# A graph and expert kernel: the first graph's order and magnitudes rebuilt, the last graph's sums shared out

## The reference

```
xn = layernorm(x);  H = (adj != 0);  w = adj[0, :]
D = 1/(H w);  B = 1/(column counts of H)
conv(h, W, b) = D * (H (B * (H^T (h W^T)))) + b
h  = relu(conv(xn, W1, b1))                 # 256 -> 512
h  = layernorm(h) * gamma + beta
x1 = x + conv(h, W2, b2) + xn               # 512 -> 256
x2 = layernorm(x1)
logits = x2 rw + rb;  mask = softmax over the two largest of 4
comb = sum_e mask_e * silu(x2 ew_e + eb_e)
y  = x2 + comb ow + ob
out = x1 + nw * y / sqrt(mean(y*y) + eps)
```

## Time and profile before

| what | value |
|---|---|
| median of 3 runs | 729.49 us (727.12 to 731.59) |
| the profiled execution | 727.4 us, its span 725.9 us |
| TensorE busy | 685.4 us (94% of the span) |
| VectorE busy | 622.8 us (86%) |
| ScalarE busy | 528.7 us (73%) |
| GpSimd busy | 342.7 us (47%) |
| share of the chain that ended last | PE 87%, DVE 5%, ACT 3%, DMA 1% |

### The profile page before, as it was taken

The page is one execution under the profiler, slowest core; times in us unless marked ns, Lnnn a source line. Parts: engine busy times, 40 slices in busy tenths (PEclk is TensorE's granted clock), DMA queues, the critical chain, the costliest instruction groups (busy, mean ns, idle before and its releaser), DMA issues.

```text
span 725.9 us, 15857 instructions
## 1 busy us (share of the span) xinstructions
PE 685.4 (94%) x5197; PEld 475.7 (66%) x5197; DVE 622.8 (86%) x1544; ACT 528.7 (73%) x1091; POOL 342.7 (47%) x731
## 2 busy tenths in 40 slices
PE   3777999999999999999999999999999999999982
PEld 2464485866758586775858577685857668585672
DVE  3987799898989989898989989898998989898676
ACT  4567868688696868778686877869686786967563
POOL 4142625456373545646354554635355563634433
PEclk9999999999999999999999999999999999999997
DMA  8547449575665938566583947657394756537312
GB/s 284 190 77 242 92 106 235 93 236 117 210 141 136 230 63 256 112 212 134 153 203 61 274 99 227 120 173 173 83 260 90 236 111 197 121 77 184 59 30 59
DMA packets 42591, 111.72 MB, mean 154 GB/s; under 512 B 4161, under 2 KB 5313, under 8 KB 42561
## 3 DMA queue, kind: packets, MB, share of 16 engines
q0 software_dynamic: 13536, 41.42, 32.8%
q1 hardware_dynamic: 29024, 69.92, 27.4%
HBM read 69.91 MB, written 16.25 MB: 119 GB/s over the span
## 4 chain that ended last, share of the span: by engine, by line
PE 87%; DVE 5%; ACT 3%; DMA 1%; issue 1%; POOL 1%; SPq 0%; POOLq 0%; DVEq 0%; ACTq 0%
PE bank L1310 16%; PE bank L1312 16%; PE bank L1311 16%; PE bank L1395 7%; PE bank L1396 7%; PE bank L1421 7%; PE bank L1453 4%; PE bank L1454 4%; PE bank L1364 4%; PE bank L1357 2%; PE bank L1412 2%; DMA b1b<-b 1%; PE bank L1466 1%; PE bank L1345 0%; ACT x L591 0%
## 5 line engine op out<-in xcount | busy, mean ns | idle before, releaser
L1310 PE MATMUL bank<-xth,ewh 128*128 128x512 f16 (+1 forms) x272 | 100.4, 369 | 2.6 <-DVE ewl L827 2.6
L1311 PE MATMUL bank<-xtl,ewh 128*128 128x512 f16 (+1 forms) x272 | 100.3, 369 | 0.0
L1312 PE MATMUL bank<-xth,ewl 128*128 128x512 f16 (+1 forms) x272 | 100.3, 369 | 0.0
L536 ACT ACTIVATE silu<-bank,ebcol,ksc 128x512 f32<-128x512 f32 x120 | 89.7, 769 | 7.7 <-PE bank L1312 4.0
L399 POOL TENSOR_TENSOR comb<-comb,silu 128x1024 f32<-128x1024 f32 x30 | 74.3, 2478 | 0.6 <-DVE silu L904 0.6
L1310 PE MATMUL bank<-w2h,hnth 128*128 128x256 f16 x256 | 70.3, 275 | 0.1
L1311 PE MATMUL bank<-w2l,hnth 128*128 128x256 f16 x256 | 70.2, 274 | 0.0
L1312 PE MATMUL bank<-w2h,hntl 128*128 128x256 f16 x256 | 70.2, 274 | 0.0
L926 DVE SCALAR_TENSOR_TENSOR hntl<-bank,hnth 128x512 f16<-128x512 f32 x64 | 42.7, 687 | 26.8 <-ACT hnth L554 25.6
L1453 PE MATMUL bank<-xsh,h 128*128 128x256 f16 x256 | 59.0, 279 | 3.1 <-DVE xsl L809 2.4
L904 DVE TENSOR_TENSOR silu<-silu,bank 128x1024 f32<-128x1024 f32 x45 | 54.7, 1216 | 7.9 <-ACT silu L536 7.8
(11 more groups left out here) (273 smaller groups left out, 2072.7 us busy)
## 6 DMA issues: line engine op xcount, KB each, us to landing
adjin<-adj SPq DMA_DIRECT2D x16, 1024.0 KB, 5.4
adjtin<-adjt SPq DMA_DIRECT2D x16, 1024.0 KB, 7.9
xin<-x SPq DMA_DIRECT2D x16, 512.0 KB, 7.1
xb<-xn SPq DMA_DIRECT2D x16, 512.0 KB, 4.1
xb<-x POOLq DMA_DIRECT2D x16, 512.0 KB, 8.9
xb<-b POOLq DMA_DIRECT2D x16, 512.0 KB, 5.4
xb<-vadd POOLq DMA_DIRECT2D x16, 512.0 KB, 4.5
out<-x SPq DMA_DIRECT2D x15, 512.0 KB, 4.9
```

Source lines behind the costliest of these rows:

```text
L536: af(silu[:, i % 4, :], bank[E_BANK[i]][:, :], ACT.Silu, bias=ebcol[:, i:i + 1], scale=ksc[:, 2:3]).then_inc(silu_dn, 1)
L1310: mm(outp, lh, rh, start=first, stop=False)
L1311: mm(outp, lh, rl, start=False, stop=False)
L1312: return mm(outp, ll, rh, start=False, stop=last)
```

## The change

In the opening of graph 0, SP loads adj, W1 and adjt right behind x, and gamma, W2, beta and b1 after them. TensorE starts with 18 products that nothing reads (`keep_busy`), and has two groups of 5 of them later. x is normalized and split by halves (`first_x`, `first_lo`), the aggregation takes the halves as they come (`first_aggregation`), and the column counts of H are made by TensorE as products with a column of ones (`count_products`, for graphs 0 and 1). `w2g` is made by GpSimd. The magnitudes of W1, `w2g` and the expert weights are no longer maxima: ScalarE sums absolute values in one instruction (`sum_abs`, with an accumulator); for the output and router weights VectorE takes the largest absolute value directly. The W2 scale, the fourth `z_part`, `bias_rows`, `v_part`, x of graph 1 and the expert weights' split stand elsewhere in the order; `ewh` is made in graph 0 and `ewl` ahead of `xtl` in graph 1. The steady passes keep their instructions.

In the tail, GpSimd makes y * nw for graph 14 (`yw_dn`) and ScalarE multiplies by the root (`finish`), where VectorE did both; the first half's sum over experts is one step on GpSimd and two on VectorE; the second half has two steps on GpSimd and the last one on VectorE by tiles of 128 nodes; the split, the output products and y follow by tiles. The first expert's high products stand ahead of the router.

```diff
-            for dst, src in ((bet[:, :], beta), (gam[:, :], gamma),
-                             (w2f[:, :, :], w2t.rearrange("(k p) f -> p k f", p=P))):
+            sp.dma_start(adjin[:, :, :], adj[0].rearrange("(t p) e -> p t e", p=P)).then_inc(adj_in, 16)
+            sp.dma_start(w1f[:, :, :], w1t.rearrange("(k p) h -> p k h", p=P)).then_inc(a_in, 16)
+            sp.dma_start(adjtin[:, :, :], adjt[0].rearrange("(t p) c -> p t c", p=P)).then_inc(adjt_in, 16)
+            for dst, src in ((gam[:, :], gamma), (w2f[:, :, :], w2t.rearrange("(k p) f -> p k f", p=P)),
+                             (bet[:, :], beta), (b1b[:, :], b1.to_broadcast([P, DH]))):
                 sp.dma_start(dst, src).then_inc(b_in, 16)
-            sp.dma_start(adjin[:, :, :], adj[0].rearrange("(t p) e -> p t e", p=P)).then_inc(adj_in, 16)
-            for dst, src in ((w1f[:, :, :], w1t.rearrange("(k p) h -> p k h", p=P)),
-                             (b1b[:, :], b1.to_broadcast([P, DH]))):
-                sp.dma_start(dst, src).then_inc(a_in, 16)
-            sp.dma_start(adjtin[:, :, :], adjt[0].rearrange("(t p) c -> p t c", p=P)).then_inc(adjt_in, 16)
...
             prep_x(0, again=False)
+            gp.wait_ge(b_in, 64)
+            tt(w2g[:, :, :], w2f[:, :, :], gam[:, :].unsqueeze(2).to_broadcast([P, KH, D]), ALU.mult).then_inc(w2g_dn, 1)
...
-                        gp.wait_ge(b_scale, 1)
-                    scale_dn(g)
+                        gp.wait_ge(a_scale, 1)
+                    scale_dna(g)
+                    if ffn:
+                        scale_dnb(g)
                 if prep and ffn:
...
                     if not ffn:
+                        gp.wait_ge(b_scale, 1)
+                        scale_dnb(g)
                         add_x(g)
+                        prep_x(g + 1)
                     add_b2(g)
                 if ffn:
                     add_up(f, 2)
                 if conv:
...
                 roots_y(LAST - 1, ALL, 0)
 
-                s = slice(0, T_ROW)
-                for e in range(1, NE):
-                    gp.wait_ge(comb_st, 7 * LAST + e + 1)
-                    if e > 1:
-                        gp.wait_ge(last_sum, e - 1)
-                    tt(comb[:, :, s], comb[:, :, s], last_silu(e)[:, :, s], ALU.add).then_inc(last_sum, 1)
+                gp.wait_ge(y_dn, 2 * LAST)
+                gp.wait_ge(out_st, 32 * (LAST - 1))
+                tt(yf[:, :, :], y[:, :, :], nwb[:, :].unsqueeze(1).to_broadcast([P, CT, D]), ALU.mult).then_inc(yw_dn, 1)
+
+                s0, s1 = slice(0, T_ROW), slice(T_ROW, 2 * T_ROW)
+                gp.wait_ge(comb_st, 7 * LAST + 2)
+                tt(comb[:, :, s0], comb[:, :, s0], last_silu(1)[:, :, s0], ALU.add).then_inc(last_sum, 1)
+                gp.wait_ge(comb_st, 7 * LAST + 6)
+                tt(comb[:, :, s1], comb[:, :, s1], last_silu(1)[:, :, s1], ALU.add).then_inc(last_sum, 1)
+                gp.wait_ge(comb_st, 7 * LAST + 7)
+                gp.wait_ge(last_sum, 2)
+                tt(comb[:, :, s1], comb[:, :, s1], last_silu(2)[:, :, s1], ALU.add).then_inc(last_sum, 1)
...
+            def sum_abs(col, src):
+                n = src.shape[1] * src.shape[2]
+                return af(silu[:, :, :].rearrange("p k n -> p (k n)")[:, 0:n], src[:, :, :].rearrange("p k n -> p (k n)"),
+                          ACT.Abs, accum_out=mags[:, col:col + 1])
...
+            def first_x():
+                act.wait_ge(xrs_st, 4)
+                for j in range(2):
+                    s = slice(CG * j, CG * j + CG)
+                    for t in range(CG * j, CG * j + CG):
+                        af(xn[:, t, :], xin[:, t, :], ACT.Identity, bias=xnb[:, t:t + 1],
+                           scale=xrs[:, t:t + 1]).then_inc(xn_dn, 1)
+                    act.wait_ge(xn_dn, CG * j + CG)
+                    af(xsh[:, s, :], xn[:, s, :], ACT.Copy, scale=XS).then_inc(xs_hi if j else x0_hi, 1)
...
+            first_x()
+            act.wait_ge(tables, 16)
+            act.wait_ge(a_in, 16)
+            sum_abs(W1, w1f).then_inc(a_mag, 1)
...
+                        act.wait_ge(a_mag, 1)
+                        act.wait_ge(w2g_dn, 1)
+                        sum_abs(W2, w2g).then_inc(b_mag, 1)
...
+                if conv and not ffn:
+                    hnt_part(act, g, 0)
+                    setup_hi(b_scale, ((w2g, w2h, W2),), b_hi)
+                    relu(act, g, 3)
+                    hnt_part(act, g, 1)
...
+                        act.wait_ge(b_mag, 1)
+                        act.wait_ge(c_in, 16 * 6)
+                        sum_abs(EX, ewf).then_inc(ew_sum, 1)
...
+                    else:
+                        bias_rows(act, g)
...
+                            if not ffn:
+                                prep_x(g + 1, range(e, e + CG))
...
-                    setup_hi(c_scale, ((rwf, rwh, RW), (owf, owh, OW)), c_hi)
+                    setup_hi(c_scale, ((rwf, rwh, RW), (ewf, ewh, EX), (owf, owh, OW)), c_hi)
...
-                if prep:
-                    count_edges(act, g, 1 - odd)
+                if prep and ffn:
+                    count_edges(act, g, 1 - odd, late)
...
+            def last_ct(act, h, t):
+                c = slice(T_ROW * h, T_ROW * h + T_ROW) if h == 0 else slice(P * t, P * t + P)
+                act.wait_ge(half_dn, 1 if h == 0 else t)
                 af(cth[:, :, c], comb[:, :, c], ACT.Copy, scale=ksc[:, 5:6]).then_inc(ct_hi, 1)
+
+            def finish(act, t):
+                act.wait_ge(yw_dn, 1)
+                act.wait_ge(rr_st, 2 * LAST)
+                af(yf[:, t, :], yf[:, t, :], ACT.Copy, scale=yrr[:, t:t + 1]).then_inc(yf_dn, 1)
...
+                for t in range(1, CT):
+                    finish(act, t)
+                for t in range(CG, CT):
+                    last_ct(act, 1, t)
...
+            def first_lo(j):
+                s = slice(CG * j, CG * j + CG)
+                dve.wait_ge(xs_hi if j else x0_hi, 1)
+                STT(xsl[:, s, :], xn[:, s, :], XS, xsh[:, s, :], ALU.mult, ALU.subtract).then_inc(xs_lo if j else x0_lo, 1)
...
+            def degrees(g, odd, counted_by_pe):
+
+                if counted_by_pe:
+                    dve.wait_ge(deg_rdy, g + 1)
+                else:
+                    dve.wait_ge(deg_dn, 4 * g - 4)
+                TS(dmax[:, :], bank[DEG_BANK][:, DEG] if counted_by_pe else deg[:, :], 1.0, None, ALU.max).then_inc(be_max, 1)
...
+            prep_h(0, again=False)
+            first_lo(0)
+            degrees(0, 0, True)
+            first_lo(1)
...
-                    setup_lo(c_hi, 2, ((rwf, rwh, rwl, RW), (owf, owh, owl, OW)), c_lo)
+                    setup_lo(c_hi, 1, ((rwf, rwh, rwl, RW),), c_lo)
...
+                    if not ffn:
+                        d_vector(g)
...
+                if conv and ffn and not late:
+                    setup_lo(c_hi, 2, ((ewf, ewh, ewl, EX),), c_lo)
...
-                        setup_scale_b()
-                        d_vector(g)
-                    dve.wait_ge(dn_scaled, 2 * g + 1)
+                        dve.wait_ge(b_in, 64)
+                    dve.wait_ge(dn_scaled, (2 * g if ffn else g) + 1)
...
+                    if not ffn:
+                        v.memset(spare[:, :], 0.0)
+                        h_aggr(g, 1)
+                        h_stats(g, 2)
+                        dve.wait_ge(hbn_dn, 4 * g + 3)
+                        v.memset(spare[:, :], 0.0)
+                        h_aggr(g, 2)
+                        setup_scale_b()
                     z_part(g, 3)
-                    h_aggr(g, 1)
-                    if not ffn:
...
+                    else:
+                        hnt_part(g, 0)
...
+                if conv:
+                    hnt_part(g, 3)
+                if ffn:
+                    combine_sum(f)
+                if ffn:
+                    ct_part(f, 0)
+                if conv:
+                    v_part(g, 0)
+                    if not ffn:
+                        largest(c_turn, slice(EX, RW + 1), 2, c_top)
...
+            def last_pair_up():
+                c = slice(0, T_ROW)
+                dve.wait_ge(comb_st, 7 * LAST + 4)
+                TT(last_silu(2)[:, :, c], last_silu(2)[:, :, c], last_silu(3)[:, :, c], ALU.add).then_inc(last_pair, 1)
...
+            def first_half_sum():
+                c = slice(0, T_ROW)
+                dve.wait_ge(last_pair, 1)
+                dve.wait_ge(last_sum, 1)
+                TT(comb[:, :, c], comb[:, :, c], last_silu(2)[:, :, c], ALU.add).then_inc(half_dn, 1)
...
+            def last_add(t):
+                c = slice(P * t, P * t + P)
+                dve.wait_ge(comb_st, 7 * LAST + 8)
+                dve.wait_ge(last_sum, 3)
+                TT(comb[:, :, c], comb[:, :, c], last_silu(3)[:, :, c], ALU.add).then_inc(half_dn, 1)
...
+                last_pair_up()
                 last_weigh(1, 0)
-                finish(LAST - 1, (2, 3), False, False)
+                first_half_sum()
```

(132 more changed lines are left out.)

199 lines of the change are left out of this document (70 added, 129 removed).

## The result

759.6 us (median of 4 runs, 758.4 to 760.3) against 728.8 (727.1 to 731.6): ratio 1.042, 95% interval 1.039 to 1.044. The change makes the kernel 31 us slower. The profiled execution has a span of 758.8 us, 32.9 more than before, and takes 760.3 in all.

The account below looks back on a forecast made before the run. TensorE, busy almost throughout the steady passes, was taken as the bound, so only the ends could gain: start 6.3 plus tail 0 from 727.4 gives 721.1, 723.2 on the median's scale, stated as 723.0; range 718.5 to 727.

Parts of the forecast that it names:

- nothing of the diff touches those passes: Steady passes, 75.2 to 691 us, TensorE busy 614.4 of 615.8: all new branches lie outside them, so no change there.
- The rival on the other side: Steady passes: VectorE starts them 2.6 late and never recovers, TensorE waiting in each; 737 at 1 us a pass, chance 0.05.
- the rival without locks: Opening and tail: VectorE and GpSimd don't hold each other up, 0.5 and 2.1 more gained; 720.0, chance 0.27.
- the lock of the tail: Tail: GpSimd's product `yw` holds VectorE's `mask` 2.2 us, cancelling a gain of 2.1; taken as 0, bounds -2.1 and +0.6.
- the last step of the sum: Conversion of 721.1, the profiled execution's scale, to the runs' median, 2.1 higher: 723.2, stated as 723.0.
- Opening of graph 0: Start of graph 0: shorter path to the first W1 products, at 21.7 instead of 27.02, gain 5.3.
- Lock of the opening: Opening of graph 0: GpSimd's `prep_h` may hold up VectorE's `xnb` if adj lands before 8.6; 0 to 1.0, taken 0.5.
- Loads: Opening rival: adj and adjt land at 11.5 and 17 as before, counts wait, gain only 3; 726.5, chance 0.11.
- the rival of a falling clock: Opening: TensorE's clock falls between warm-up and aggregation, which again runs slower, gain 4.3; 725, chance 0.12.
- Rest of graph 0: From W1 products to `x1_half(0)`: GpSimd's queue of additions to xb holds it; 57.27 becomes 53.5, gain 3.8.
- Graph 1: From `x1_half(0)` to graph 1's W1 products: 13.9 instead of 17.9, W1 products at 67.4, 7.8 ahead of 75.16.
- The 1.0 for VectorE's lateness: Graph 1: route and mask come 2.6 later relative to TensorE, missing transpositions; cost 1.0, bounds 0 and 2.

Follow-up runs that it names:

- e1: Changed kernel with ten instructions of waits on a reached semaphore ahead of VectorE's first instruction, its loop at 329 instead of 319: 719.3 us, ratio 0.987.
- e15: Changed kernel with VectorE's loop moved by waits to 329 and all 28 `keep_busy` products left out: 720.8 us.
- e12: Changed kernel with five wait instructions (loop at 324), GpSimd's tail product y*nwb ahead of the x2 addition, and graph 0's additions to xb issued earlier: 713.9 us.
- e8: Changed kernel with VectorE's loop moved by waits to 329 and GpSimd's tail product y*nwb put ahead of the x2 addition: 717.2 us, ratio 0.984.
- e14: Changed kernel with a single wait instruction ahead, VectorE's loop of 261 at 320: 747.4 us, with shorter pauses.
- e3: Changed kernel with 128 wait instructions ahead of VectorE's first instruction, its loop at 447: 769.7 us, with pauses.
- e11: Changed kernel with no waits ahead, VectorE's loop one instruction shorter (260) at 319: 760.9 us, with all five pauses.
- e13: Kernel before the change with 114 wait instructions ahead, VectorE's loop at 443 in the list and 447 on the engine: 774.7 us, with pauses.
- e7: Changed kernel with 261 wait instructions ahead of VectorE's first instruction, its loop at 580: 743.9 us, no pauses.

## Why the prediction was wrong

**The step that failed** is in its first paragraph: "nothing of the diff touches those passes". That holds for the operations, but for one instruction more in VectorE's loop, and between the marks e1 takes 630.8 us where the kernel before takes 634.8. But a loop has a place in the instruction stream too, and fourteen instructions less ahead of it, as the engine counts (ten in the list), moved it from a good one to a bad one. The prediction had this at nothing without a reason; it costs 41.5 us between the marks, more than everything that the forecast weighed. The rival on the other side had TensorE waiting in each pass of the loop because VectorE began late. It waited at five jumps back because VectorE's code was not there; the sign was right by accident, and the mechanism fell in e1, where VectorE begins as late and loses nothing by it. Nothing in the trace of before shows a cost of the place; what it had was the queue of instructions with only 2 of its 15 packets between 200 and 640 us (the changed kernel has 26 there), and the program's list would have given the shift.

**The rest is best read in e1**, which is the change without that accident: 719.3, at the lower end of the range and 3.7 below the forecast. It is near the rival without locks (720.0), but not by its mechanism, since the lock of the tail did bite. Some 1.6 of the 3.7 are the change: 1.8 more at the start, 0.2 less in the tail. The other 2 are in the last step of the sum, which put some 2 on top of 721.1 because the profiled execution of before lay that far under its median; in e1 the profiled execution (719.5) lies 0.2 over it.

- *Opening of graph 0*: W1 products at 21.14 in the changed kernel and 21.29 in e1 (forecast 21.7). Counts, aggregation at 11.18 and at 0.11 spacing were right. Of the half microsecond, 0.4 is an error of addition: the prediction's own steps behind 15.6 add up to 21.3.
- *Lock of the opening*: 0.5 was taken off for it and should not have been. `prep_h` did hold a GpSimd instruction, but it began at 8.80 and `xnb` was out at 8.60; it was `wr` that took 1.26 (0.32 before), which nobody waits for.
- *Loads*: this rival was wrong. adj released `prep_h` at 8.80 instead of 11.78, and `prep_ht` began at 12.86 without a wait for adjt.
- *Clock*: the warm-up does what the forecast assumed (e15), and the rival of a falling clock was wrong.
- *Rest of graph 0*: 53.0 in the changed kernel and 53.2 in e1, held by the vadd transfer (forecast 53.5, so held). The path was right, the number partly by luck: `add_x`, `add_b2` and `add_v` went out at 34.6, 40.5 and 46.8 (forecast 36.4, 42.6 and 48.5), and the last transfer then took 6.2 to land (forecast 4.8 to 5.1). e12 shows that the order on GpSimd's queue alone held this place.
- *Graph 1*: W1 products at 66.65 in the changed kernel and 66.80 in e1 (forecast 67.4). The 1.0 for VectorE's lateness was mis-sized: in e1 these products start 8.4 ahead of the earlier trace rows, and 8.1 of it is left at the last `x1_half` (684.0 for 692.1), so it cost 0.3. Start gain 8.1 for 6.3: 0.6 by the earlier products, 0.7 by the lateness, 0.5 by the lock of the opening.
- *Tail*: forecast 0, with `mask` held to 2.2. It took 2.25, and the tail is 34.0 in e1 and 33.5 in the changed kernel, for 33.8. Right, in mechanism and in size; e8 shows that the lock cost 2.1 to the end.

## What to carry to other kernels

Before a change is judged, look whether its loops kept their place: idle time with releaser "issue" at the first instruction of a loop body, once for each jump back, and packets in the instruction queue inside the loop are the sign, and a few waits on a reached semaphore ahead of the loop both test and mend it. Count as the engine does; here each `accum_out` added an instruction that the program's list lacks. By bounds 128 apart a loop of up to 257 instructions can't reach four pieces, wherever it begins; that is worked out from these runs and was not tried. Where a big product on GpSimd can run while VectorE waits or reads from the banks, put it there: the place of one instruction was worth 2.1 us here, and issuing a chain of three transfers in an idle gap 3.3.

## What the runs showed of the hardware

- VectorE's code comes in pieces of 128 instructions, as far as all 17 places of the table show. A loop of 260 or 261 costs nothing in three pieces; in four it costs VectorE 4.7 to 6.9 us for each jump back, with some five packets of 8.2 KB, and this kernel 5.7 (e14) to 8.3 us (the changed kernel) between the marks, both against e1.
- With the loop 2 ahead of a bound the pauses are 6.4 to 6.9 us (changed, e3, e11, e13), 1 ahead of it 4.7 to 5.1 (e14). Why one instruction makes 1.7 us of difference stays open.
- ScalarE shows no idle time of this kind in the changed kernel, e1, e3, e12 or e13, and GpSimd none above 0.6 us. Their loops were not moved on purpose, and they are short: 190 and 157 instructions in the list, 206 on ScalarE with its accumulator reads.
- 256 waits on a reached semaphore held VectorE's first instruction until 14.1 us (e3, 128 instructions) and 522 until 27.4 us (e7, 261), some 0.10 for each instruction of two.
